# A batch in another order, with a query stack in the maxima's banks, merged ranks, and padding written in blocks during the attention

## The chip, the core and the metric

The kernel runs on one NeuronCore of a Trainium2 chip. The core has five engines, each with a program of its own, which meet only at semaphores: TensorE (PE: matmuls and transposes into PSUM), VectorE (DVE), ScalarE (ACT), GpSimd (POOL) and SyncE (SP), which here only issues DMAs. The metric is the device time of one execution in microseconds, as a median over runs. Lower is better.

## The reference

One layer with gated cross attention and a routed feed-forward part, in fp32, on 16 batches of 256 tokens with 256 features:

```python
x = x + tanh(g_xattn[0]) * attention(layernorm(x), ctx, ctx, ...)   # 16 heads of 16, softmax(q k / 4) v, then wo
x = x + tanh(g_ffn[0]) * ffn(layernorm(x), ...)
# ffn:
bids = sigmoid(x @ conf_w.T + conf_b) * wealth                # 8 experts
top_bids, selected = top_k(bids, 2)
routing_weights = softmax(top_bids)                           # over the two chosen
out = sum over the chosen experts of weight * (silu(x @ gate.T) * (x @ up.T)) @ down.T
```

## The kernel before

**Two stages.** The attention stage goes over the 16 batches; the expert stage goes over the tokens that were routed to each of the 8 experts. Between them lies a list of rows in DRAM, `dispatched`, with a region of 4096 + 256 rows of 272 floats for each expert: 256 normed features, 8 weights, the token's number. GpSimd scatters each batch's rows there with four indirect DMAs (L1211), to places that the routing has counted out. The expert stage reads a region in tiles of 256 rows, so what follows the last real row up to the end of its tile must be padding, rows of zero weight that point at a spare output row. The kernel before writes this padding in two ways: 32 rows at the head of each region early in the program (L435), and 256 rows behind the last real row of each, when the counts are known (`pad_experts`, L375, four experts by SyncE and four by GpSimd).

**A batch.** The program of an iteration `b` works on several batches at a time: scores, exps and weighing for `b`, the maxima (which are subtracted in the softmax) for `b + 1`, projections of Q and K for `b + 2`, output projection, residual and second layernorm for `b - 1`, ranks and rows of the dispatch for `b - 2`. The order is written out by hand, once for each engine, in a function `body`; the batches 0, 1, 14 and 15 are written out separately and the twelve between run in a loop of two. `ahead`, `nxt`, `back` and `late` say which of those parts an iteration has.

**PSUM.** `scores` holds one unit of work at a time: a pair of heads (`S0` to `S7`), or a stack of Q or K (`K0`, `K1`, `Q0`, `Q1`: the projection split into a high part and a rest, and put in the layout of heads). TensorE writes a unit, ScalarE reads it (exps or `read_stack`) and counts `unit_read`; TensorE's next unit waits for that. `maxps` holds the score maxima's own scores; VectorE reduces them (L984) and counts `max_taken`. `pv` holds the weighed values of one group of heads, which ScalarE copies out (`read_pv`, L818). `misc` has three banks that go round among all other products.

**The inputs of a batch.** SyncE loads the context (`load_ctx`, L394): batches 0 and 1 ahead of the loop, 2 in iteration 0, 3 and 4 in iteration 1, and then `b + 3` in iteration `b`. TensorE projects K of batch `b + 2` in iteration `b` (`project_k`, L493, for `b < 2`, from the load itself; later from a copy that GpSimd has split, `split_ctx`). At the end of iteration `b` SyncE moves the maxima's row into the queries of `b + 1` (`store_shift`, L422), for which `score(b + 1, 0)` waits. SyncE issues in the order of its program.

**From attention to experts.** After the last batch its rows are normed, routed and scattered, the counts are made (L1155), GpSimd adds the first outputs to `out` (`add_first`, L1884, one waiting for the other), SyncE loads the first full tile of rows (L1425), GpSimd copies it (L1882), and TensorE turns it (L1468) and begins gate and up (L1485).

## Time and profile before

| | before |
|---|---|
| time, median of 3 runs | 1084.73 us (1083.60 to 1086.69) |
| time of the profiled execution | 1083.07 us |
| its span from the first to the last instruction | 1081.4 us |
| TensorE busy, share of the span | 1001.3 us, 93% |
| VectorE, ScalarE, GpSimd busy | 610.8, 502.0, 366.3 us |
| mean traffic of the DMA engines | 71 GB/s |
| attention stage | up to about 444 us |
| first full tile of an expert begins | 483.24 us |

All times in rows are microseconds from the span's start. An engine's row tells when an instruction began, how long it took, the engine, the line, what it wrote from what, and in brackets how long the engine had been idle before it and what ended that. Ends of matmuls are modelled, so a small gap in TensorE is read from the starts. SyncE's rows are the issuing of DMAs, not their transfer.

### The profile page before, as it was taken

What the parts mean: (1) busy time and instruction counts of PE and PEld (TensorE: products, weight loads), DVE (VectorE), ACT (ScalarE), POOL (GpSimd) and SP (SyncE); (2) the same over time, 40 slices, a digit from 0 to 9 for tenths busy, and PEclk for the clock granted to TensorE, in tenths of its full rate; (3) what the DMA queues carried; (4) which work ended last, traced back from release to release, by engine and by line L of the source; (5) the groups of instructions that cost most, each with busy time, mean ns of one, the idle gap of its engine ahead of it and who ended that gap; (6) DMA issues with size and microseconds to landing.
All of it is one profiled execution on the core that took longest, in us unless ns stands there. A gap on an engine that the chain in (4) does not pass through costs nothing.

```text
span 1081.4 us, 25127 instructions
## 1 busy us (share of the span) xinstructions
PE 1001.3 (93%) x8750; PEld 855.2 (79%) x8750; DVE 610.8 (56%) x1519; ACT 502.0 (46%) x796; POOL 366.3 (34%) x439
## 2 busy tenths in 40 slices
PE   5789999999999997759999999999999999999993
PEld 4556777777777765448999999999799999999993
DVE  3556777777777776455544444444554444444452
ACT  4366777777777774334323232332433323233321
POOL 1124555555555552443322212121332212122121
PEclk8799999999999999869999999999999999999997
DMA  8000111111111119258712111121262212121211
GB/s 254 27 22 22 43 45 47 41 41 41 43 51 58 41 39 371 77 182 323 256 25 40 25 35 35 25 37 23 42 229 49 37 23 40 20 40 23 37 35 17
DMA packets 48338, 77.30 MB, mean 71 GB/s; under 512 B 8616, under 2 KB 42152, under 8 KB 44456
## 3 DMA queue, kind: packets, MB, share of 16 engines
q0 software_dynamic: 18080, 50.15, 16.7%
q1 hardware_dynamic: 30216, 26.62, 8.3%
q8 instruction: 23, 0.38, 0.1%
q14 instruction: 19, 0.16, 0.0%
HBM read 52.09 MB, written 24.40 MB: 71 GB/s over the span
## 4 chain that ended last, share of the span: by engine, by line
PE 81%; ACT 5%; issue 4%; DVE 3%; POOL 3%; DMA 1%; SPq 1%; POOLq 1%; ACTq 0%; DVEq 0%
PE gate L1485 17%; PE up L1485 17%; PE down L1499 11%; PE down L1501 6%; PE pv L590 4%; PE scores L579 4%; PE misc L486 4%; PE scores L540 3%; PE maxps L554 2%; PE misc L513 2%; PE misc L522 2%; POOL K_rest L1204 2%; ACT probs L771 1%; PE misc L624 1%; PE turned L1468 1%
## 5 line engine op out<-in xcount | busy, mean ns | idle before, releaser
L1937 POOL DMA_INDIRECT out<-y,token x64 | 100.9, 1577 | 424.8 <-DVE y L1806 323.8
L1696 ACT ACTIVATE silu<-gate 128x512 f32<-128x512 f32 x128 | 76.8, 600 | 281.6 <-PE up L1485 281.6
L984 DVE TENSOR_REDUCE max_neg<-maxps 128x4 f32<-128x1024 f32 x128 | 156.5, 1222 | 60.2 <-PE maxps L554 60.2
L1485 PE MATMUL gate<-x_hi,w_split 128*128 128x256 f32 x1024 | 185.0, 282 | 2.0 <-DVE x_lo L1772 1.6
L1797 DVE TENSOR_TENSOR h<-silu,up 128x512 f32<-128x512 f32 x128 | 88.1, 688 | 174.8 <-ACT silu L1696 174.8
L1499 PE MATMUL down<-w_split,h_hi 128*128 128x512 f32 x512 | 185.9, 398 | 0.0
L1485 PE MATMUL up<-x_hi,w_split 128*128 128x256 f32 x1024 | 184.4, 282 | 0.0
L771 ACT ACTIVATE probs<-scores 128x1024 f32<-128x1024 f32 x124 | 127.2, 1026 | 80.5 <-PE scores L579 79.5
L1485 PEld LDWEIGHTS gate<-x_hi,w_split 128*128 128x128 f32 x1024 | 149.4, 189 | 5.5 <-issue 2.7
L1485 PEld LDWEIGHTS up<-x_hi,w_split 128*128 128x128 f32 x1024 | 148.8, 189 | 0.0
L1501 PE MATMUL down<-w_split,h_lo 128*128 128x256 f32 x512 | 144.1, 281 | 0.0
L1799 DVE TENSOR_TENSOR h_lo<-h,h_hi 128x512 fp32r<-128x512 f32 x128 | 89.0, 696 | 89.5 <-ACT h_hi L1699 89.5
L1699 ACT ACTIVATE h_hi<-h 128x512 fp32r<-128x512 f32 x128 | 81.0, 633 | 96.8 <-DVE h L1797 96.8
L1499 PEld LDWEIGHTS down<-w_split,h_hi 128*128 128x128 f32 x512 | 96.2, 188 | 17.6
L1485 PE MATMUL up<-x_lo,w_split 128*128 128x256 f32 x512 | 103.2, 283 | 0.0
L1485 PE MATMUL gate<-x_lo,w_split 128*128 128x256 f32 x512 | 103.0, 283 | 0.0
L1501 PEld LDWEIGHTS down<-w_split,h_lo 128*128 128x128 f32 x512 | 96.4, 188 | 0.0
L1485 PEld LDWEIGHTS up<-x_lo,w_split 128*128 128x128 f32 x512 | 79.2, 189 | 0.0
L1485 PEld LDWEIGHTS gate<-x_lo,w_split 128*128 128x128 f32 x512 | 78.5, 189 | 0.0
L1211 POOL DMA_INDIRECT dispatched<-row,posi x64 | 63.9, 999 | 28.7 <-issue 17.3
L590 PE MATMUL pv<-probs,values 128*32 128x256 f32 x1024 | 69.4, 389 | 1.6 <-ACT oS L818 1.6
L579 PE MATMUL scores<-queries,keys 64*128 64x256 f32 x496 | 61.8, 328 | 8.3 <-ACT probs L771 4.3
(204 smaller groups left out, 1586.3 us busy)
## 6 DMA issues: line engine op xcount, KB each, us to landing
stage<-gate_up_T POOLq DMA_DIRECT2D x20, 1024.0 KB, 8.1
stage<-down_T POOLq DMA_DIRECT2D x10, 1024.0 KB, 11.1
xg<-dispatched SPq DMA_DIRECT2D x34, 272.0 KB
ctxT<-ctxT SPq DMA_DIRECT2D x17, 256.0 KB, 2.8
x_all<-x SPq DMA_DIRECT2D x16, 256.0 KB, 5.2
out<-x_all SPq DMA_DIRECT2D x16, 256.0 KB, 2.2
dispatched<-pads SPq DMA_DIRECT2D x4, 272.0 KB, 3.6
dispatched<-pads POOLq DMA_DIRECT2D x4, 272.0 KB, 4.3
```

Of the source, the lines that this page charges most:

```text
L579: last = mm(to[:, u * QT + t, :], k[par][r, pair, t * P:(t + 1) * P], q[par][r, pair, :], start=True, stop=True)
L590: last = mm(pv[j * SLOT:(j + 1) * SLOT, 0:SEQ], v[par][:, t, g * HPG + j, :], probs[g % 2][:, j, t, :], start=t == 0, stop=t == QT - 1)
L771: nc.scalar.activation(probs[g % 2][:, at:at + HPP].rearrange("p u t s -> p (u t) s"), home(b, pair), ACT.Exp).then_inc(s["unit_read"], 1)
L984: V.tensor_reduce(to, maxps[:], AX.X, ALU.max, negate=True).then_inc(s["max_taken"], 1)
L1485: last = mm(bank[:, i, :], into_inner(w, pair, mat)[:, c, cols], r[:, c, :], start=m == 0, stop=m == len(terms) - 1)
L1499: mm(down[t][:].rearrange("p (n d) -> p n d", n=2), h_hi[:, i, rows], split[:, :, cols], start=i == 0, stop=False, skip_group_check=True)
L1501: last = mm(down[t][:, 0:D], h_lo[:, i, rows], hi[:, cols], start=False, stop=i == IC - 1, skip_group_check=True)
L1696: nc.scalar.activation(silu[pair % 2][:], gate[pair % 2][:], ACT.Silu).then_inc(s_silu, 1)
L1699: nc.scalar.activation(h_hi[:, 2 * pair:2 * pair + 2, :], h[pair % 2][:], ACT.Copy).then_inc(s_hhi, 1)
L1797: V.tensor_tensor(h[pair % 2][:], silu[pair % 2][:], up[pair % 2][:], ALU.mult).then_inc(s_made, 1)
L1799: V.tensor_tensor(h_lo[:, 2 * pair:2 * pair + 2, :], h[pair % 2][:], h_hi[:, 2 * pair:2 * pair + 2, :].bitcast(fp32), ALU.subtract).then_i ...
L1937: pool.indirect_dma_start(out, bass.IndirectOffsetOnAxis(token[:, t:t + 1], axis=0), y[:, t, :], None, compute_op=ALU.add).then_inc(s_adde ...
```

## The change

Five things are changed together.

1. The padding. The 32 rows at the head of each region and the `pad_experts` at the end both go. Instead SyncE writes whole blocks of 256 rows in each of the 8 regions, from iteration 0 on: two blocks in iterations 0 and 1, one in each of 2 to 14, at the end of its `body` behind `store_shift`. A block is 8 DMAs of 272 KB. A scatter of batch `b` waits until `b + 1` blocks are written.
2. The order of an iteration from the fifth score on: `weigh(1)` goes ahead of `K0`, the Q projection ahead of score 5, `turn_x2` ahead of score 6, score 7 behind `weigh(2)`, `K1` behind the logits. ScalarE's order follows: `read_pv(1)` ahead of `K0`, `norm_x2` ahead of exps 5, `x2T` ahead of exps 7, the sigmoid ahead of `K1`. VectorE's `positions` go ahead of the sixth maximum.
3. The stack `Q0` goes to the banks of `maxps`, which are free once the maxima are turned. `Q1` then waits for the reading of `K1` alone.
4. The ranks of both token tiles are made by two matmuls of 16 columns in place of five of 8. For this VectorE adds the first tile's marks to the running count before the ranks (`macc[:, 1]`) and not behind them.
5. After the last batch, the first product of expert 2 is made ahead of turning the last rows, and the second between that and the logits; the counts' integer copy, which only the padding read, goes.

```diff
-            for e in range(EXPERTS):
-                sp.dma_start(disp[e * REGION:e * REGION + FIRST], pads[0:FIRST]).then_inc(s["first_rows_padded"], 16)
+
+            def pad_block(n):
+
+                rows = disp.rearrange("(e n) d -> e n d", e=EXPERTS)[:, bass.ds(n * SEQ, SEQ)].rearrange("e (t p) d -> p e t d", p=P)
+                for e in range(EXPERTS):
+                    sp.dma_start(rows[:, e], pads[:].unsqueeze(1).to_broadcast([P, QT, ROW])).then_inc(s["blocks_padded"], 16)
+
+            def pad_blocks(b):
+
+                if isinstance(b, int) and b < 2:
+                    pad_block(2 * b)
+                    pad_block(2 * b + 1)
+                elif isinstance(b, int) and b == BATCHES - 2:
+                    pad_block(BATCHES)
+                elif not is_last(b):
+                    pad_block(b + 2)
...
                 if nxt:
                     store_shift(b + 1, 1 - par, use)
+                pad_blocks(b)
...
-            return (lambda: store_residual(BATCHES - 1, EPILOGUE), lambda: pad_experts(sp, range(EXPERTS // 2)))
+            return (lambda: store_residual(BATCHES - 1, EPILOGUE),)
...
-            def stack(b, what, c, n):
+            def stack(b, what, c, n, to=None):
...
-                write_unit(n)
+                if to is None:
+                    to = scores
+                    write_unit(n)
...
-                for t in range(QT):
-                    mm(use.bank("RK")[:, t, 0:EXPERTS], before[:], m12[:, t, :], start=True, stop=False)
-                    if t == 1:
-                        mm(use.bank("RK")[:, t, 0:EXPERTS], ones[:], m12[:, 0, :], start=False, stop=False)
-                    last = mm(use.bank("RK")[:, t, 0:EXPERTS], ones[:], macc[:], start=False, stop=True)
-                last.then_inc(s["misc_written"], 1)
+                mm(use.bank("RK")[:, :, 0:EXPERTS], before[:], m12[:], start=True, stop=False)
+                mm(use.bank("RK")[:, :, 0:EXPERTS], ones[:], macc[:], start=False, stop=True).then_inc(s["misc_written"], 1)
...
+                weigh(b, par, 1)
                 stack_ahead("K0")
-                weigh(b, par, 1)
-                max_of_next(5)
-                score(b, par, 5)
                 if ahead:
                     project_q(use)
-                score(b, par, 6)
+                score(b, par, 5)
+                max_of_next(5)
                 if back:
                     turn_x2(b - 1, 1 - par, use)
+                score(b, par, 6)
                 max_of_next(6)
+                weigh(b, par, 2)
                 score(b, par, 7)
-                weigh(b, par, 2)
                 max_of_next(7)
-                stack_ahead("K1")
                 if back:
                     logits(use)
+                stack_ahead("K1")
                 if nxt:
                     turn_maxima(b + 1, use)
                 stack_ahead("Q0")
...
                 read_pv(b, 0)
                 if ahead:
                     read_whole(xT[:], "TX", use)
+                read_pv(b, 1)
                 stack_ahead("K0")
-                exps(b, 5)
                 if back:
                     norm_x2(b - 1, 1 - par)
-                read_pv(b, 1)
-                exps(b, 6)
+                exps(b, 5)
                 if ahead:
                     read_q(b + 2, use)
-                exps(b, 7)
+                exps(b, 6)
                 if back:
                     read_whole(x2T[:], "TX2", use)
+                exps(b, 7)
                 read_pv(b, 2)
-                stack_ahead("K1")
                 if back:
                     sigmoid(use)
+                stack_ahead("K1")
                 stack_ahead("Q0")
                 stack_ahead("Q1")
...
-                V.tensor_tensor(m12[:], m1[:], m2[:], ALU.add).then_inc(s["masks_ready"], 1)
+                V.tensor_tensor(m12[:], m1[:], m2[:], ALU.add).then_inc(s["masks_made"], 1)
+                dve.wait_ge(s["masks_made"], b + 1)
+                if not is_first(b):
+                    dve.wait_ge(s["rows_ready"], b)
+                V.tensor_tensor(macc[:, 1, :], macc[:, 0, :].bitcast(fp32), m12[:, 0, :].bitcast(fp32), ALU.add).then_inc(s["masks_ready"], 1)
...
                 max_of_next(4)
-                max_of_next(5)
                 if late:
                     positions(b - 2, par, use)
+                max_of_next(5)
                 max_of_next(6)
...
                 alone.wait_ge(s["rows_ready"], b + 1)
+                alone.wait_ge(s["blocks_padded"], b * (16 * EXPERTS) + 16 * EXPERTS)
...
             early_product(1, 1)
+            early_product(2, 0)
             turn_last_x2()
+            early_product(2, 1)
             last_logits()
-            early_product(2, 0)
-            early_product(2, 1)
             last_ranks()
```

## Rows read from the trace of the kernel before

**Rows 1.** Windows: stretch, length, busy us (instructions), granted clock, DMA share, GB/s.

```profile
16.00:28.00 12.00, 9.27 (x57) 6.84 (x56) 3.29 (x4) 7.26 (x12) 0.00 (x0) 0.72 0.92 295
...
48.15:54.95 6.80, 4.72 (x16) 3.46 (x16) 0.89 (x1) 0.42 (x2) 1.37 (x4) 0.50 0.13 40
...
98.30:398.00 299.70, 291.81 (x2823) 214.28 (x2821) 233.96 (x689) 223.12 (x348) 159.50 (x224) 1.00 0.13 43
404.70:421.40 16.70, 12.85 (x133) 8.11 (x131) 11.98 (x37) 8.59 (x15) 7.21 (x12) 1.00 0.98 404
467.50:475.50 8.00, 4.67 (x171) 4.01 (x162) 2.69 (x5) 4.28 (x5) 6.64 (x8) 0.71 0.94 323
474.80:488.40 13.60, 6.24 (x28) 5.88 (x29) 6.69 (x9) 2.60 (x3) 4.21 (x6) 0.50 0.73 236
```

**Rows 2.** Timeline of PE in the first batches: K projections of batches 2, 3.

```profile
50.23 3.78 PE L486 MATMUL misc<-ctxT,wk_s 128*128 128x256 f32 x8 [2.46 <-DMA ctxT<-ctxT]
...
77.16 1.99 PE L486 MATMUL misc<-ctxT,wk_s 128*128 128x256 f32 x8
```

**Rows 3.** Timeline of PE, first full tile of rows.

```profile
480.55 1.09 PE L1468 MATMUL turned<-idn,rows 128*128 128x128 f32 x4 [8.38 <-POOL rows L1882]
```

**Rows 4.** Timeline of SP in the first batches: issue of DMAs.

```profile
43.33 4.16 SPq L436 DMA_DIRECT2D dispatched<-pads  x8
...
70.63 1.33 SPq L427 DMA_DIRECT2D queries<-max_rows  x2
72.06 3.08 SPq L398 DMA_DIRECT2D ctxT<-ctxT  x2
```

**Rows 5.** Timeline of POOL between attention and experts.

```profile
470.13 2.94 POOL L381 DMA_DIRECT2D dispatched<-pads  x4
473.38 1.68 POOL L1885 DMA_INDIRECT out<-y_first,first_token  x1 [0.30 <-issue]
478.11 1.64 POOL L1885 DMA_INDIRECT out<-y_first,first_token  x1 [3.05 <-DMA out<-y_first,first_token]
479.52 0.88 POOL L1882 COPY rows<-xg 128x544 f32<-128x544 f32 x1
```

**Rows 6.** View of line 381, the large pads: issue in ns, landing in us.

```profile
L381 SPq DMA_DIRECT2D dispatched<-pads x4: 372/379/407, 466.7 to 470.6; - x4
...
DMA to landing us min/median/max: 2.3/4.2/4.8
```

**Rows 7.** View of line 388, the sixteen loads of x.

```profile
L388 SPq DMA_DIRECT2D x_all<-x x16: 434/469/925, 0.9 to 21.8; - x16
...
DMA to landing us min/median/max: 2.8/5.2/6.4
```

**Rows 8.** Timeline of PE in a full batch: five rank matmuls, K0.

```profile
235.61 0.25 PE L632 MATMUL misc<-m,before 128*128 128x8 f32 x1
...
236.06 0.25 PE L635 MATMUL misc<-macc,ones 128*128 128x8 f32 x1
236.66 0.39 PE L540 MATMUL scores<-K_high,picks_K high 64*128 64x256 f32 x2 [0.36 <-POOL K_rest L1204]
```

**Rows 9.** Timeline of ACT in the same batch.

```profile
236.10 0.38 ACT L818 ACTIVATE oS<-pv 128x256 f32<-128x256 f32 x1
...
237.44 1.11 ACT L778 ACTIVATE keys<-scores,ones_row 128x1024 fp32r<-128x1024 f32 x1 [0.47 <-PE scores L540]
...
240.07 1.08 ACT L794 ACTIVATE row<-x_all,shift,rstd 128x256 f32 x2
```

**Rows 10.** Timeline of PE in batch 14, where no K0 follows the ranks.

```profile
410.45 1.07 PE L590 MATMUL pv<-probs,values 128*32 128x256 f32 x16 [0.69 <-ACT oS L818]
```

**Rows 11.** DMA issues: count and median us from issue to landing.

```profile
out<-y_first,first_token POOLq DMA_INDIRECT x8, 3.2
```

**Rows 12.** Timeline of SP: loads of expert rows.

```profile
476.36 14.92 SPq L1425 DMA_DIRECT2D xg<-dispatched  x3
```

**Rows 13.** Timeline of DVE: splitting of weights before the first tile.

```profile
473.66 4.63 DVE L1811 TENSOR_TENSOR w_split<-stage,w_split 128x1024 fp32r<-128x1024 f32 x4 [1.05 <-ACT w_split L1710]
```

More of the change, by code:

```diff
@@ L287, in attention_stage @@
         STACKS = ["K0", "Q0", "K1", "Q1"]
+        BESIDE = "Q0"
         def units_before(b):
@@ L309, in home @@
             return scores[:]
+        beside = maxps[:].rearrange("p u t s -> p (u t) s")
         def first_stack_unit(b, what):
@@ L373, in attention_over @@
             eng.wait_ge(s["x2_stored"], 16 * BATCHES)
-        def pad_experts(eng, experts):
-            eng.wait_ge(s["pads_loaded"], 16)
-            eng.wait_ge(s["counted"], 1)
-            for e in experts:
-                n = eng.value_load(counts[0:1, e:e + 1], min_val=0, max_val=TOKENS)
-                eng.dma_start(disp[bass.ds(n + e * REGION, TILE)].rearrange("(t p) d -> p t d", p=P),
-                              pads[:].unsqueeze(1).to_broadcast([P, TT, ROW])).then_inc(s_padded[2 * e // EXPERTS], 16)
         def sync_attention(sp):
@@ L539, in stack @@
                             r = slice(half * STACK, (half + 1) * STACK)
-                            last = mm(scores[:, half * QT + i, :], picks[f"{what} {part}"][r, i, :], source[what][r, c, :],
+                            last = mm(to[:, half * QT + i, :], picks[f"{what} {part}"][r, i, :], source[what][r, c, :],
                                       start=part == "high", stop=part == "rest")
@@ L641, in known_counts @@
                 use.free(pe, "KNOWN")
-                mm(use.bank("KNOWN")[:, 0, 0:EXPERTS], ones[:], macc[:], start=True, stop=True).then_inc(s["misc_written"], 1)
+                mm(use.bank("KNOWN")[:, 0, 0:EXPERTS], ones[:], macc[:, 0, :], start=True, stop=True).then_inc(s["misc_written"], 1)
             pe.wait_ge(s["first_loaded"], 16 * NFIRST)
@@ L680, in stack_ahead @@
                 def stack_ahead(what):
-                    if ahead:
-                        stack(b + 2, what[0], int(what[1]), unit(b, what))
+                    if ahead and what == BESIDE:
+                        stack(b + 2, what[0], int(what[1]), None, beside)
+                    elif ahead:
+                        stack(b + 2, what[0], int(what[1]), unit(b, what) - (1 if UNITS[UNITS.index(what) - 1] == BESIDE else 0))
                 if isinstance(b, int) and b < 2:
@@ L752, in count_rows @@
                 EPILOGUE2.free(pe, "COUNT")
-                mm(EPILOGUE2.bank("COUNT")[:, 0, 0:EXPERTS], ones[:], macc[:], start=True, stop=True).then_inc(s["misc_written"], 1)
+                mm(EPILOGUE2.bank("COUNT")[:, 0, 0:EXPERTS], ones[:], macc[:, 0, :], start=True, stop=True).then_inc(s["misc_written"], 1)
             pe.wait_ge(s["w_split"], 2)
@@ L869, in stack_ahead @@
                     if ahead:
-                        read_stack(par, what[0], int(what[1]), unit(b, what))
+                        read_stack(par, what[0], int(what[1]), unit(b, what), beside if what == BESIDE else None)
                 exps(b, 0)
@@ L1032, in positions @@
                 dve.wait_ge(s["second_ready"], b + 1)
-                link = chain(dve, "rows_chain", 14, b, behind=1)
+                link = chain(dve, "rows_chain", 13, b, behind=1)
                 link(V.tensor_tensor(t8[:], m1[:], u8[:], ALU.mult))
@@ L1156, in count @@
                 EPILOGUE2.written(dve, "COUNT")
-                link = chain(dve, "count_chain", 2, 0)
-                link(V.tensor_copy(counts[:], EPILOGUE2.bank("COUNT")[:, 0, 0:EXPERTS]))
+                link = chain(dve, "count_chain", 1, 0)
                 link(V.tensor_scalar(tiles[:], EPILOGUE2.bank("COUNT")[:, 0, 0:EXPERTS], float(TILE - 1 - FIRST), None, ALU.add))
@@ L1258, in scatter_last @@
                 scatter(BATCHES - 1, (BATCHES - 1) % 2)
-                pad_experts(pool, range(EXPERTS // 2, EXPERTS))
             over_batches(pool, body)
```

33 lines of the change are left out of this document (14 added, 19 removed).

## Prediction

> **What bounds the kernel now.** I read the windows first. In the twelve full batches in the middle (98.3 to 398 us) TensorE is busy 291.81 of 299.70 us, at the full clock (1.00), against 234, 223 and 160 us for VectorE, ScalarE and GpSimd [rows 1]. A batch takes 24.98 us, TensorE waits in 0.66 us of it, and no other engine comes near. So in a full batch the order of TensorE's work is worth at most its waits, plus matmuls that vanish. Then I read TensorE's timeline for longer waits. There are two that the change touches: 2.46 us before the K projection of batch 2, for a context load [rows 2], and 8.38 us between the attention and the first full expert tile, for GpSimd's copy of the rows [rows 3]. SyncE's timeline says why the first exists: the load of batch 2's context stands behind eight pad writes that take 4.16 us to issue [rows 4]. GpSimd's says why the second does: pads, two accumulating writes one after the other, then the copy [rows 5]. Durations are from the profiled execution, 1083.07 us for a span of 1081.4; the median of the runs is 1.66 above it. About 0.3% (3.25 us) can be told from no change.
>
> **First batches, what is removed.** The eight small pad writes (43.33 to 47.49) go, so the load of context 2 is issued 4.2 us earlier and has landed before TensorE asks: -2.46 [rows 2, 4]. The half clock (1.2 GHz, 0.50) of 48.15 to 54.95 lies around that wait, and TensorE is busy 4.72 of its 6.8 us [rows 1]. The same projection took 3.78 us there and 1.99 at 2.4 GHz [rows 2]. If the clock stays up, at most another 2.2 us return; if not, nothing. I take 0.8. Sum: -3.3 (-2.5 to -4.7).
>
> **First batches, what is added.** This decides the sign. `pad_blocks(0)` writes two blocks, 16 DMAs of 272 KB, right after the shift rows of batch 1 (issued 70.63 to 71.96). The very next thing in SyncE's program is `load_ctx(3)`, now issued at 72.06 [rows 4], and TensorE projects K of batch 3 at 77.16 [rows 2]. A context load is there 2.6 us or so after its issue (issued right behind 47.49, it releases TensorE at 50.23) [rows 2, 4], so today there are some 2.5 us to spare. With 16 pads ahead:
> issue alone: 0.379 us each [rows 6], 16 make 6.1, so the load is issued at 78.1 and lands at 80.6: 3.4 us late even if the pads' bytes took no time.
> bytes: 16 x 278.5 KB = 4.46 MB. SyncE's transfers land in the order of issue and pile up: of the 16 loads of x the last was issued at 21.8 and landed 6.4 us later, where the quickest took 2.8 [rows 7]. The stretch in which these 1 KB rows stream moved 295 GB/s with the DMA engines 0.92 busy; the one in which today's large pads and scatters run, 323 at 0.94; the expert weights' large rows, 404 at 0.98 [rows 1]. The pads are rows of 1088 bytes, so 323 is nearest. A lone pad lands after 2.3 us [rows 6], the other fifteen at 0.86 each, the context behind them 0.81: 72.0 + 2.3 + 12.9 + 0.8 = 88.0, or 10.8 us after 77.16. With 404 GB/s it is 8.1, with 295 12.2.
> The Trainium skill says the same in "DMA: Bandwidth & Descriptors", "Queues, rings and completion order": all DMAs issued by SyncE share one row of rings, and each DMA engine consumes its ring in order. The piling up of the loads of x agrees [rows 7]. Its "Specifications" give about 358 GB/s per core for HBM; by that the fifteen pads would take 11.7 instead of 12.9 us, and the stall be 9.5.
> TensorE's program is in order, so the scores, the weighing and all later work of batch 1 stand behind `project_k(3)`. Both shifts move together, so the -3.3 doesn't change the stall. After such a wait TensorE comes back at 1.2 GHz: the window from 474.8 to 488.4 is at 0.50 throughout, and covers the second half of the 8.38 us wait and 7.9 us after it [rows 1, 3]. 3 to 7 us at a pace 1.9 times slower lose 1.5 to 3.4; I take 2.4. Sum: +13.2 (9.6 to 15.6). Batch 2 gets two blocks as well, but the context load behind them is for GpSimd's split near the end of that batch, over 20 us after its issue, as in all later batches, where 8 pads (6.9 us) lie ahead of it. The residual's store behind them is read by nobody until the end. Scatters now wait for their blocks, which were issued two batches before: nothing.
>
> **Full batches.** Five rank matmuls, 0.11 us apart, become two [rows 8]: -0.33. K0 waits 0.36 us for K_rest [rows 8]; behind `weigh` it won't. But `weigh(1)` now stands directly behind the ranks, and needs the bank that ScalarE empties at 236.10 + 0.38 = 236.48 [rows 9]. With the hand-over that is 236.6, and the pair of K0 and `weigh` starts at 236.66 today [rows 8]: both gains sink into a new wait of some 0.8 us. The trace has this order already, in batch 14, which has no K0: `weigh` behind the ranks waits 0.69 us for ScalarE's oS [rows 10]. What follows: K0 goes from about 237.6, its eviction starts 0.78 later as now (236.66 to 237.44) and takes 1.11, then `norm_x2`, which now stands before exps(5), takes 1.08 [rows 9], to 240.5. score(5), behind K0 (0.67) and the Q projection (1.92), is at 240.2; its exps runs from about 240.8 to 241.8, and score(6), for which TensorE is free at 241.5, waits 0.3. Against these stand the waits that go: 0.2 or so for Q1, since Q0 has banks of its own, and smaller ones. I take 0.0 per batch, between -0.2 and +0.3, for twelve -2.4 to +3.6. At the far end, if every wait of TensorE went and the ranks too, it would be 0.66 + 0.33 a batch, -12. The extra VectorE sum ahead of the ranks has its cover in the same wait; without it it would cost its own length. `positions` ahead of max 5 runs while TensorE projects Q. In batches 14 and 15 the same trades occur once each, and block 16 competes with the last weight loads: +0.3 (-0.5 to +1).
>
> **Between attention and experts.** GpSimd loses four pads, 2.94 us from 470.13 [rows 5]; its first accumulating write starts at 470.4, lands after 3.2 us, the median of these writes [rows 11], instead of 4.0 without pads in the way, the second follows at 474.3, and 1.4 later the copy: 475.7 instead of 479.52. SyncE's row load (476.36) no longer waits for pads, only for the last scatter, and is issued by 473.5 [rows 12]. Then the tile could start 3.8 earlier. The first x_lo needs VectorE, which splits weights until 478.29 [rows 13]; with the turn at 476.7 and ScalarE's copy behind it x_lo is due at 478.6, so that just fits. -3.8 (-2.5 to -4.2). A shorter wait also means fewer matmuls at 1.2 GHz, or the same: -0.6 (-1.5 to +1, with the moved early products, which only fill a wait of TensorE). The two fewer rank rounds and one count fewer on the last batch's chain are offset by the extra sum: -0.1. Sum -4.5.
>
> **The sum**: -3.3 + 13.2 + 0.0 + 0.3 - 4.5 = +5.7 on 1083.07, so 1088.8 for a profiled execution and 1090.4 as a median.
>
> **Rivals.**
> (1) The pads get out of the way: the load of context 3 comes only as late as the issue makes it. For it: 404 GB/s has been moved. Against: not with rows of 1 KB. Stall 3.4, clock 1.5: 1084.73 - 3.3 + 4.9 + 0.3 - 4.5 = 1082.1, inside what can't be told or just below.
> (2) The new order pays, on the other side: if `weigh(1)` didn't wait for oS, each batch would lose its 0.8 us and TensorE would go through, 12 x 0.8 = -9.6: 1080.8. It decides from 0.75 us a batch on (9.0/12, with 5.7 to make good and 3.25 to be told). For it: TensorE is the bound in every batch. Against: batch 14 shows the wait, and ScalarE's order ahead of that eviction is unchanged.
> (3) The pads disturb every batch: 2.2 MB stream in the first 9 us of each, after the shift rows (the wait for which isn't seen in any full batch) and beside scatters. If the shift rows came late by 0.5 us a batch: +6, 1096. For it: they are on the same DMA engines. Against: the pads are issued behind them.
>
> **How the numbers follow.** Forecast 0.60, with its own range of 1085 to 1096; rival (1) 0.15, (2) 0.12, (3) 0.13. The time is the forecast's, 1090.4. The range takes in most of (1) and (3) and half of (2): 1081 to 1098. Faster by over 0.3%: (2) and a third of (1), 0.16. The same: the rest of (1) and the low end of the forecast, 0.20. Slower: 0.64.
>
> **What would show it.** In the changed profile: no wait before the K projection of batch 2; before that of batch 3 a wait of 8 to 12 us for ctxT, TensorE at 0.50 behind it; batches of 24.7 to 25.2 us with a wait of 0.6 to 0.9 for oS before `weigh(1)` and none for K_rest; the wait before the first row turn down from 8.38 to 4 to 5 us. I am wrong if context 3 lands in time, or if a full batch changes by over 0.3 us.

## The result

The change made the kernel slower: 1100.93 us as a median of four runs (1097.48 to 1103.49) against 1085.71 (1083.60 to 1087.39) on the same chip, a ratio of 1.0144 with a 95% interval of 1.0118 to 1.0171. 1090.4 was predicted, with 1098 as the upper end. The profiled execution of the changed kernel took 1097.48 us with a span of 1095.7, 14.3 above the span of before. Four stretches, each from one mark on TensorE's timeline to the next, hold all of it: V of batch 2 is the first V of a full batch, "heads" is the start of the last group of transposes of `oS`, "gate" the first product of the first full tile.

| stretch | before | after | difference | predicted |
|---|---|---|---|---|
| start to V of batch 2 | 98.27 | 109.17 | +10.9 | +9.9 |
| twelve full batches | 299.73 | 302.47 | +2.7 | 0.0 |
| V of batch 14 to the heads of batch 15 | 45.19 | 50.45 | +5.3 | +0.3 |
| heads of batch 15 to the first gate | 40.05 | 35.69 | -4.4 | -4.5 |
| the rest | 598.2 | 597.9 | -0.2 | 0 |

The windows of the changed kernel, columns as in [rows 1]: the wait before K of batch 3 with what follows it, the full batches, batches 14 and 15, and the way to the first gate.

```profile
76.00:89.60 13.60, 4.32 (x14) 3.14 (x16) 0.00 (x0) 0.00 (x0) 0.00 (x0) 0.50 0.65 209
109.17:411.64 302.47, 290.17 (x2786) 211.97 (x2784) 234.62 (x688) 223.18 (x348) 160.15 (x224) 1.00 0.41 139
411.64:462.09 50.45, 36.26 (x310) 24.00 (x308) 24.92 (x90) 24.84 (x38) 20.56 (x30) 0.83 0.88 322
462.09:497.78 35.69, 20.40 (x339) 14.63 (x340) 20.88 (x91) 11.79 (x21) 14.98 (x18) 0.78 0.21 59
```

In the full batches TensorE is busy 1.7 us less than in [rows 1] (fewer rank matmuls) and the stretch is 2.7 us longer: its waits grew. In batches 14 and 15 the granted clock is 0.83.

The timeline of TensorE of the changed kernel, at the places of [rows 2], [rows 8], [rows 10] and [rows 3], and at the first score of batch 15:

```profile
47.27 1.99 PE L492 MATMUL misc<-ctxT,wk_s 128*128 128x256 f32 x8
...
85.28 3.78 PE L492 MATMUL misc<-ctxT,wk_s 128*128 128x256 f32 x8 [11.74 <-DMA ctxT<-ctxT]
...
248.50 1.07 PE L598 MATMUL pv<-probs,values 128*32 128x256 f32 x16 [0.65 <-ACT oS L824]
...
253.71 0.50 PE L587 MATMUL scores<-queries,keys 64*128 64x256 f32 x4 [0.29 <-ACT probs L777]
...
439.00 0.80 PE L587 MATMUL scores<-queries,keys 64*128 64x256 f32 x4 [5.34 <-DMA queries<-max_rows]
...
495.09 1.09 PE L1473 MATMUL turned<-idn,rows 128*128 128x128 f32 x4 [5.34 <-POOL rows L1887]
```

The wait for context 2 [rows 2] is gone, that for context 3 is new, `weigh(1)` waits for `oS` in every batch, and K0 no longer waits for `K_rest`. SyncE's timeline of the same execution tells why context 3 is late. Its issue is the row behind the sixteen pads:

```profile
67.25 1.32 SPq L418 DMA_DIRECT2D queries<-max_rows  x2
68.61 11.64 SPq L431 DMA_DIRECT2D dispatched<-pads  x16
80.35 5.33 SPq L389 DMA_DIRECT2D ctxT<-ctxT  x2
...
411.51 5.97 SPq L431 DMA_DIRECT2D dispatched<-pads  x8
422.90 0.40 SPq L445 DMA_DIRECT2D out<-x_all  x1
433.14 1.36 SPq L418 DMA_DIRECT2D queries<-max_rows  x2
```

```profile
488.18 1.61 POOL L1890 DMA_INDIRECT out<-y_first,first_token  x1 [0.30 <-issue]
492.00 1.63 POOL L1890 DMA_INDIRECT out<-y_first,first_token  x1 [2.21 <-DMA out<-y_first,first_token]
494.11 0.83 POOL L1887 COPY rows<-xg 128x544 f32<-128x544 f32 x1 [0.48 <-DMA xg<-dispatched]
```

### The profile page after: what moved, and what is told of

Same layout as the page of the kernel before. It is cut to its first block, busy times and chain, and to the rows that moved or that the text cites. A ratio compares the mean times of both kernels' runs of the same rounds, so it can differ in the third digit from the quotient of the medians.

```text
span 1095.7 us, 25472 instructions
## 1 busy us (share of the span) xinstructions
PE 999.1 (91%) x8702; PEld 852.4 (78%) x8702; DVE 611.9 (56%) x1518; ACT 502.2 (46%) x796; POOL 363.3 (33%) x435
## 4 chain that ended last, share of the span: by engine, by line
PE 80%; ACT 6%; issue 5%; DVE 3%; DMA 2%; SPq 2%; POOL 1%; ACTq 0%; DVEq 0%; POOLq 0%
PE gate L1490 17%; PE up L1490 17%; PE down L1504 11%; PE down L1506 6%; PE pv L598 6%; PE scores L587 4%; PE misc L492 4%; PE scores L548 3%; PE maxps L562 2%; ACT probs L777 2%; PE misc L519 2%; PE misc L528 2%; PE turned L1473 1%; PE misc L480 1%; ACT xn L791 1%
## 5 line engine op out<-in xcount | busy, mean ns | idle before, releaser
L587 PEld LDWEIGHTS scores<-queries,keys 64*128 64x128 f32 x496 | 38.0, 190 | 47.7 <-ACT probs L777 20.8
```

The lines of the kernel that those rows point to most:

```text
L587: last = mm(to[:, u * QT + t, :], k[par][r, pair, t * P:(t + 1) * P], q[par][r, pair, :], start=True, stop=True)
```

## The experiments

All marks are those of the table above: V of batch 2, the mean of ten periods (V of batch 4 to V of batch 14), batches 14 and 15 with TensorE's mean granted clock in them, and the tail. Ratios are to the kernel before on the same chip; a dash is a single execution.

| kernel | median us | ratio, 95% | V of batch 2 | period | 14 and 15 (clock) | tail |
|---|---|---|---|---|---|---|
| before | 1085.71 | | 98.27 | 24.88 | 45.19 (0.92) | 40.05 |
| after | 1100.93 | 1.0144 (1.0118-1.0171) | 109.17 | 25.16 | 50.45 (0.83) | 35.69 |
| pads only | 1093.75 | 1.0076 (1.0050-1.0102) | 108.78 | 24.85 | 49.52 (0.83) | 38.32 |
| order only | 1089.72 | 1.0047 (1.0033-1.0062) | 96.05 | 25.16 | 49.31 (0.80) | 41.05 |
| after, context 3 ahead | 1085.14 | 1.0006 (0.9991-1.0020) | 96.07 | 25.16 | 51.98 (0.81) | 36.56 |
| after, half the bytes | 1097.08 | - | 105.08 | 25.15 | 52.93 (0.78) | 36.62 |
| after, pads moved | 1095.23 | 1.0093 (1.0076-1.0110) | 93.40 | 25.17 | 49.80 (0.81) | 36.45 |
| before, pads moved | 1091.34 | 1.0057 (1.0035-1.0078) | 93.95 | 24.88 | 49.38 (0.79) | 36.72 |
| order, statistics later | 1098.23 | 1.0124 (1.0099-1.0149) | 98.35 | 26.09 | 45.45 (0.92) | 40.58 |
| early products only | 1085.81 | 0.9998 (0.9985-1.0012) | 98.68 | 24.88 | 45.17 (0.92) | 40.08 |
| context 2 first | 1080.51 | 0.9964 (0.9947-0.9980) | 97.29 | 24.87 | 47.35 (0.86) | 40.40 |
| before, pads spread | 1076.75 | 0.9924 (0.9902-0.9946) | 93.32 | 24.87 | 47.86 (0.82) | 36.79 |
| ranks only | 1085.65 | 1.0006 (0.9990-1.0021) | 98.87 | 24.86 | 47.39 (0.89) | 40.40 |
| order, no ranks | 1090.12 | 1.0050 (1.0033-1.0067) | 97.21 | 25.16 | 48.61 (0.83) | 41.37 |

**Pads only.** The kernel before with the blocks of padding (`pad_block`, `pad_blocks`, the wait ahead of the scatter, no `pad_experts`) and nothing else of the change.

> The kernel before with the blocks of padding alone; order, stacks and ranks stay. Theory A (the pads stand in front of other transfers of SyncE's queue and beside the weight loads of batches 14 and 15): a wait of 10 to 13 us for context 3 in batch 1, full batches of 24.9 us as before, some 5 us lost around batches 14 and 15, some 4 us won between attention and experts: 1097 us. Rival B (the new order of a batch is what costs): about the kernel before or faster, 1080 to 1086.

TensorE's timeline:

```profile
85.06 3.78 PE L489 MATMUL misc<-ctxT,wk_s 128*128 128x256 f32 x8 [11.41 <-DMA ctxT<-ctxT]
```

The wait before K of batch 3 is 11.41 us, so the blocks alone make it. The full batches keep their period (24.85), though each now moves 2.2 MB of pads: beside the attention these bytes cost nothing that a full batch shows. Batches 14 and 15 lose 4.3 us. The tail gains 1.7 where theory A had 4, and the time is 1093.75 where it had 1097.

**Order only.** All of the change but the padding.

> The kernel before with the new order, the stack in the maxima's banks and the merged ranks; padding as before. Theory A: full batches of 25.1 to 25.2 us in place of 24.9, so 3 us over twelve, no wait for context 3, the wait of 8.4 us before the first full tile stays: 1087 to 1090. Rival B: most of the 15 us is here, 1097 or more. Rival C (the pads' traffic is what makes full batches longer, and the order gains): batches of 24.9 us or less.

The whole +0.28 us a batch is here, and no wait for a context. The medians come near to adding up: 9.3 us of the first and 5.3 of this one against 15.2 of both. By stretches they don't: batches 14 and 15 lose 4.3 and 4.1 us apart and 5.3 together, and the tail changes by -1.7 and +1.0 apart and by -4.4 together. So the agreement of the medians is partly luck.

**Context 3 ahead of the pads,** in the changed kernel:

```diff
-                    sp.wait_ge(s["misc_written"], use.before)
-                    load_ctx(b + 2, par)
+                    if b == 0:
+                        sp.wait_ge(s["misc_written"], use.before)
+                        load_ctx(b + 2, par)
...
                 if nxt:
                     store_shift(b + 1, 1 - par, use)
+                if is_first(b):
+                    sp.wait_ge(s["misc_written"], ITER1.before)
+                    load_ctx(3, 1)
                 pad_blocks(b)
```

> The changed kernel, with context 3 loaded in iteration 0 ahead of the 16 pads and not behind them. Theory A: the wait for context 3 (11.7 us) and the half clock behind it are gone, 12 to 14 us: 1087 to 1089. Rival D (the pads' bytes disturb TensorE's transfers wherever they stand): context 3 still comes some 5 to 10 us late, 1095.

One DMA moved past sixteen others takes 13.1 us off the first batches (V of batch 2 at 96.07, not 109.17). The profiled execution falls by 10.4 us, to 1087.12, since batches 14 and 15 take 1.5 us more and the tail 0.9. The median falls by 15.8, to that of before. Of that, 5.4 us is not in the two profiles: the profiled run of after is the quickest of its four, and the one here lies 2.0 above the median of its ten. So the move is worth 10 to 13 us, and the rest of the change still costs 3.9 us in this profile (a span of 1085.3 against 1081.4). Timelines of SyncE and TensorE in this kernel, where the same sixteen pads now follow:

```profile
69.47 0.39 SPq L389 DMA_DIRECT2D ctxT<-ctxT  x1
69.91 11.97 SPq L431 DMA_DIRECT2D dispatched<-pads  x16
```

```profile
74.26 0.92 PE L496 MATMUL misc<-ctxT,wk_s 128*128 128x256 f32 x3
```

K of batch 3 starts at 74.26 with no wait. The pads themselves are unchanged, so it is the place in SyncE's order that costs, not the traffic beside the engines. Context and pads land in the order in which they were issued, the context at 72.32 and the pads from 73.19 to 86.40. With this the trace agrees with the Trainium skill, "DMA: Bandwidth & Descriptors", "Queues, rings and completion order", where each DMA engine takes what one issuing engine put in its ring in order.

**Half the bytes, as many DMAs.** Iteration 0 writes one block in sixteen DMAs of 136 KB, iteration 1 the other three, and the scatters wait for one block's worth of DMAs more:

```diff
+                if isinstance(n, int) and n == 0:
+                    for e in range(EXPERTS):
+                        for t in range(QT):
+                            sp.dma_start(rows[:, e, t], pads[:]).then_inc(s["blocks_padded"], 16)
+                    return
...
```

> The changed kernel, with 16 pad DMAs of half the size in iteration 0 (block 0 alone, in halves; block 1 follows in iteration 1). If the bytes in the queue make context 3 late, as predicted, the wait falls from 11.7 us to 5 to 6. If the number of DMAs does (issue), it stays at 10 to 12.

SyncE's and TensorE's timelines:

```profile
68.48 9.41 SPq L433 DMA_DIRECT2D dispatched<-pads  x16
77.99 3.28 SPq L389 DMA_DIRECT2D ctxT<-ctxT  x2
```

```profile
80.86 1.65 PE L500 MATMUL misc<-ctxT,wk_s 128*128 128x256 f32 x3 [7.47 <-DMA ctxT<-ctxT]
```

The wait is 7.47 us, between what half the bytes alone and the unchanged count alone would give. The small pads are issued and land 0.5 us apart (0.43 to 0.46 for an issue, but for the seventh of 2.02, whose cause the trace doesn't show), nearly all 1.9 to 2.2 us after their issue. The large ones pile up: the first lands after 2.3 us, the thirteenth after 4.1. So with 272 KB the draining sets the pace, with 136 KB the issuing. The prediction's two bounds, issue and bytes, are both real, and the larger one counts.

**Pads moved, in the changed kernel and in the kernel before.** Context 3 ahead of all pads; then blocks 0 and 1; 2, 3 and 4 in iteration 1 and `b + 3` in iteration `b`, from iteration 1 on ahead of the residual's store and the shift rows; none in batches 14 and 15.

```diff
...
+                if b != 0 if isinstance(b, int) else True:
+                    pad_blocks(b)
                 if back:
                     store_residual(b - 1, use)
                 if nxt:
                     store_shift(b + 1, 1 - par, use)
-                pad_blocks(b)
...
```

> The changed kernel with its padding blocks placed elsewhere in SP's order: context 3 is loaded ahead of all pads, every batch's pads stand ahead of its residual store and its shift rows and one batch earlier (blocks 0 and 1 in batch 0; 2, 3 and 4 in batch 1; block b+3 in batch b), so that none is issued in batches 14 and 15. Theory (a): the pads' traffic in batches 14 and 15 delays the x2 store and with it the shift rows of batch 15; without it the stretch from V of batch 14 to the heads of batch 15 falls from the 51.98 us of the kernel with context 3 ahead to the 49.3 of the new order alone, the wait of the first score of batch 15 falls from 5.57 to about 2.2 us, and the time is about 1082.5 us. Theory (b): the loss in batches 14 and 15 is the new order's and the clock's; the stretch stays at 51 to 52 us and the time at 1085. The mean period of the full batches stays at 25.15 to 25.16 us by both.

> The order of the kernel before, with only the padding blocks of the change and these placed as in the mended form (context 3 ahead of all pads, pads one batch earlier and ahead of the residual store and the shift rows, none in batches 14 and 15). Theory (a): the blocks cost nothing in the full batches (24.85 to 24.88 us a batch), save some 2.8 us in the first batches (K of batch 2 at about 47.4 instead of 50.23), nothing more is lost in batches 14 and 15 (45.2 us from V of batch 14 to the heads of batch 15, as before), and the tail from there to the first gate takes 38.3 instead of 40.05 us: together -4.5 us, 1080 us. Theory (b): the pads disturb batches 13 to 15 wherever they stand in SP's order, or the time won early is given back where the weight loads end: 1084 to 1088 us.

Both forecasts of the time missed, since I had made the same mistake again one place further on. Timelines of SyncE and TensorE in the second of the two:

```profile
80.48 18.75 SPq L428 DMA_DIRECT2D dispatched<-pads  x24
99.27 0.64 SPq L444 DMA_DIRECT2D out<-x_all  x1
99.95 1.51 SPq L415 DMA_DIRECT2D queries<-max_rows  x2
```

```profile
106.31 0.79 PE L590 MATMUL scores<-queries,keys 64*128 64x256 f32 x4 [10.68 <-DMA queries<-max_rows]
```

Twenty-four pads now stand ahead of the shift rows of batch 2, and the first score of batch 2 waits 10.68 us (11.10 in the other kernel). It also failed in batches 14 and 15: with no pad issued there the stretch still takes 49.38 us in this kernel, at a clock of 0.79, where theory (a) had 45.2. In the changed kernel theory (a) came close there: the wait of the first score of batch 15 fell to 2.12 us and the stretch from 51.98 to 49.80, for 49.3. Both windows are at a clock of 0.81, so the pads' traffic in these batches costs about 2.2 us.

**Statistics later.** Order only, with `stats_x(b + 2)` behind `max_of_next(0)` on VectorE.

> The new order and merged ranks without the padding blocks (1089.72 us), with one edit on VectorE: the LayerNorm statistics of x two batches ahead (five instructions, 1.6 us) move from ahead of the reading of V and the first maxima to behind the first maxima. Theory (a): the chain on VectorE over the batch boundary (turned maxima, first choice, statistics, V, first maxima) sets when the second maxima's matmuls may begin, so the period of a full batch falls from 25.155 to between 24.9 and 25.05 us and the time to 1086.5 to 1088.5 us. Theory (b): the period is set inside the batch by ScalarE's read of the first attention output ahead of the weighing (0.65 us wait) and by the exponentials; then what is won at the boundary is lost at that wait, the period stays within 0.03 of 25.155 and the time within 1 us of 1089.7.

Neither held: the period grew to 26.09. The timelines of VectorE show why, first of order only, then of this kernel:

```profile
270.58 0.41 DVE L994 CAST max_rows<-misc 16x256 fp32r<-16x256 f32 x1 [0.75 <-PE misc L567]
...
274.50 0.25 DVE L940 BATCH_NORM_AGGREGATE mv<-stats 128x2 f32<-128x6 f32 x2 [0.26 <-DVE stats L935]
274.66 0.74 DVE L979 TENSOR_TENSOR values<-misc,bv_s 128x256 f32<-128x256 f32 x2
```

```profile
226.69 0.41 DVE L994 CAST max_rows<-misc 16x256 fp32r<-16x256 f32 x1 [0.75 <-PE misc L567]
...
228.75 0.17 DVE L1012 TENSOR_TENSOR m<-u,r 128x16 f32<-128x16 f32 x1
230.56 0.76 DVE L979 TENSOR_TENSOR values<-misc,bv_s 128x256 f32<-128x256 f32 x2 [1.64 <-PE misc L525]
231.23 1.23 DVE L987 TENSOR_REDUCE max_neg<-maxps 128x4 f32<-128x1024 f32 x1
232.38 0.42 DVE L935 BATCH_NORM_STATS2 stats<-x_all 128x6 f32 x1
```

V isn't made yet when the first choice is done. The statistics had filled a wait of VectorE for TensorE, and behind the maxima they delay the second ones: TensorE waits 0.7 us for VectorE's maxima in eleven batches, where order only has one such wait. VectorE takes V 3.87 us after the turned maxima (the cast at 226.69) here, and 4.08 in order only, so its chain holds TensorE there by 0.2 us at most; it is not what a move of 1.6 us can mend.

**Ranks only, and the order without the ranks.** The two halves of the trade inside a batch.

> The kernel before with the merged ranks alone (two rank matmuls a batch for five, and one sum more on VectorE). Theory (a): what TensorE saves, 0.33 us a batch, goes into the wait for K_rest behind it (0.36 to about 0.69 us), the period stays at 24.87 us within 0.03 and the time within 1.5 us of 1085. Theory (b): the saved matmuls shorten the batch by 0.33 us, twelve times 4 us: 1081.

> The new order of a batch with the query stack in the maxima's banks, without the merged ranks and without the padding blocks. Theory (a): the period of the new order is set by ScalarE's read of the first attention output and by the exponentials behind it, so that three more rank matmuls only fill the wait of 0.65 us before the weighing (0.3 left): the period stays at 25.13 to 25.17 us and the time within 1.5 us of the 1089.7 of the order with merged ranks. Theory (b): TensorE's own work sets it: 25.45 to 25.5 us and about 1093.5.

Theory (a) held both times. TensorE's timeline of ranks only, then of the order without the merged ranks:

```profile
237.19 0.39 PE L540 MATMUL scores<-K_high,picks_K high 64*128 64x256 f32 x2 [0.68 <-POOL K_rest L1203]
```

```profile
236.47 1.07 PE L595 MATMUL pv<-probs,values 128*32 128x256 f32 x16 [0.31 <-ACT oS L825]
```

Three rank matmuls less turn 0.36 us of waiting for `K_rest` [rows 8] into 0.68. Three more turn 0.65 us of waiting for `oS` into 0.31. The period doesn't move in either, so those matmuls lay in a wait both before and after.

**Early products only.** The kernel before with the last edit of the change (item 5) and nothing else.

> The kernel before with only the last edit of the change: the turn of the last x2 and the last logits stand one place later among the early products of the experts on TensorE. Theory (a): the tail's gain in the changed kernel comes from this move and the padding together; alone it lets TensorE run up the clock ahead of the logits but the wait for the counts and the shared pad stores remains, so the time is 1083 to 1085 us with 39 to 40 us from the heads of batch 15 to the first gate. Theory (b): the move alone makes the gain: 36 to 37 us for that stretch and 1080.5 to 1081.5 us. Theory (c): it delays the last logits by a product (about 2 us) and nothing gives it back: 1086 us.

Nothing is won: 40.08 us of tail. That is theory (a); the time, 1085.81, lies 0.8 above its range and within 0.2% of before.

**Context 2 first.** The kernel before, with one move on SyncE:

```diff
-            for e in range(EXPERTS):
-                sp.dma_start(disp[e * REGION:e * REGION + FIRST], pads[0:FIRST]).then_inc(s["first_rows_padded"], 16)
...
                     load_ctx(b + 2, par)
+                    if b == 0:
+                        for e in range(EXPERTS):
+                            sp.dma_start(disp[e * REGION:e * REGION + FIRST], pads[0:FIRST]).then_inc(s["first_rows_padded"], 16)
```

> The kernel before with one move on SP: the load of context 2 stands ahead of the eight first-row pads instead of behind them. Nothing is added and nothing is left out, so that only the wait of 2.46 us before the K projection of batch 2 goes. Both theories: K of batch 2 at about 47.4 instead of 50.23 us and everything up to V of batch 14 some 2.5 to 4.5 us earlier. Theory (a): batches 14 and 15 are held by the transfers beside them, which don't change, so they take 45.2 us from V of batch 14 to the heads of batch 15 as before, and the time falls by 2.5 to 4.5 us, to 1080.6 to 1082.6. Theory (b): in batches 14 and 15 TensorE's clock is what moves, and it comes out otherwise as soon as the same work comes some us earlier or later, with no transfer added: that stretch takes 47 to 50 us, and the time stays within 2 us of 1085.

Faster by 0.36%, with no wait for context 2. V of batch 14 comes 1.1 us earlier in the profiled execution, not 2.5 to 4.5. The median, 1080.51, is near theory (a). Yet in the profiled execution, of 1083.96 us, batches 14 and 15 took 47.35 us at 0.86, as theory (b) had it, with no transfer added anywhere. Six of its twelve runs took 1078.86 to 1079.23 us, with a granted clock of 0.969 to 0.972 over the whole run, and six 1081.79 to 1084.34, with 0.962 to 0.967, the profiled one among the latter.

**Pads spread.** The order of before, with the blocks behind loads that are due and ahead of nothing that is: 0 and 1 behind context 2, block 2 behind context 3, 3 and 4 behind context 4, then `b + 3` behind the context load of iteration `b`.

```diff
...
                     load_ctx(b + 3, 1 - par)
+                    pad_block(b + 3)
...
```

> The order of the kernel before with the padding blocks of the change where SP has nothing behind them that is due: blocks 0 and 1 right behind context 2, block 2 behind context 3, blocks 3 and 4 behind context 4, block b+3 behind the context load of batch b, none in batches 14 and 15. By the theory that only what stands behind the pads in SP's order is late, no context and no shift rows are waited for in the first four batches (V of the first full batch at 93.5 to 94 us, 4.5 us earlier than before), the period stays 24.88 us, and the tail from the heads of batch 15 to the first gate takes 36.7 to 38.3 us instead of 40.05. With 45.2 us in batches 14 and 15 that gives 1077 to 1079 us; with the 49.4 us that the two kernels with pads and the old order took there, 1081 to 1083. Rival: 4.46 MB of pads between 43 and 56 us disturb batch 1 itself: over 1086.

1076.75 us, 0.76% faster than before, the fastest kernel of this study. Its windows: full batches, batches 14 and 15, the tail, and the stretch at half clock in batches 14 and 15.

```profile
93.32:392.93 299.61, 291.75 (x2823) 214.30 (x2821) 234.02 (x689) 223.13 (x348) 159.23 (x224) 1.00 0.41 132
392.93:440.79 47.86, 38.47 (x316) 25.27 (x314) 24.87 (x89) 24.62 (x38) 21.10 (x31) 0.82 0.64 246
440.79:477.58 36.79, 22.50 (x345) 15.51 (x346) 20.29 (x91) 11.80 (x21) 15.71 (x19) 0.80 0.21 61
411.40:428.40 17.00, 15.11 (x93) 9.22 (x86) 6.60 (x26) 6.86 (x10) 5.61 (x7) 0.50 0.79 312
```

The rival didn't come: 4.46 MB of pads between 43 and 60 us delay nothing. The first batches give 4.95 us, the tail 3.3, and batches 14 and 15 take 2.7 back.

**Four kernels profiled again,** to learn whether the program or the execution sets the clock in batches 14 and 15.

> The kernel before, unchanged, profiled once more. In its first profile batches 14 and 15 took 45.19 us from V of batch 14 to the heads of batch 15 at a mean granted clock of 0.92. Theory (a): the stretch is fixed by the program: 45.1 to 45.3 us at 0.92 again. Theory (b): TensorE's clock comes out otherwise from execution to execution: any length from 45 to 49 us, with the same waits and a clock of 0.79 to 0.92.

> The changed kernel, unchanged, profiled once more; its first profile had 50.45 us in batches 14 and 15 at a granted clock of 0.83, and a wait of 5.34 us of the first score of batch 15 for its shift rows. Theory (a): 50.2 to 50.7 us again. Theory (b): 48 to 54 us with the clock; the wait for the shift rows stays between 4.3 and 5.6 us, since the transfers make it. By both the wait of 11.7 us before the K projection of batch 3 and the period of 25.16 us stay within 0.3 and 0.02.

> The kernel before with context 2 ahead of the first-row pads, profiled once more; its first profile took 1083.96 us with 47.35 us in batches 14 and 15 at 0.86, while six of its twelve runs took 1078.9 to 1079.2. Theory (a): 47.3 us again. Theory (b): the clock differs: about 45.2 us at 0.92 where the run is one of 1079 us, 47 to 48 where it is one of 1082 to 1084.

> The new order and merged ranks without the padding blocks, profiled once more; its first profile had 49.31 us in batches 14 and 15 at a granted clock of 0.80. Theory (a), the new order itself costs 4 us there: 49.3 us again. Theory (b), it costs 0.3 us at an equal clock: 45.4 us where the clock is 0.92, 48 to 50 where it is 0.80 to 0.83. By both the period is 25.155 us within 0.02.

| kernel | first profile | second profile |
|---|---|---|
| before | 45.19 (0.92) | 45.67 (0.93) |
| after | 50.45 (0.83) | 51.95 (0.81) |
| context 2 first | 47.35 (0.86) | 47.31 (0.86) |
| order only | 49.31 (0.80) | 49.76 (0.81) |

The two profiles of one program lie within 1.5 us of each other, where the programs lie between 45 and 52. So much of the stretch comes with the program. Neither theory holds alone, though: before and after missed the narrow ranges of theory (a), and the other two kernels came back at the clock of their first profiles, where both theories say much the same. That executions of one program differ too is told by the granted clock of whole runs: the kernel before, on the chip of context 2 first, took from 1081.59 us at 0.972 to 1088.98 at 0.964. The second profile of the changed kernel has its waits again: 11.76 us for context 3, 5.59 for the shift rows. By stretches, the second profile of after against that of before gives +7.4, +2.7, +6.3 and -3.2 us, so batches 14 and 15 are again far from the +0.3 that was predicted.

## Why the prediction was right and wrong

**First batches: right.** +9.9 predicted, +10.9 measured. Context 3 behind sixteen pads was the step that decided the sign, and with that one load moved the first batches lose nothing. The stall was put at 10.8 us from bytes at 323 GB/s and came to 11.74; the K projection behind it ran at 1.2 GHz for 3.78 us as the one of [rows 2] does. Rival (1), that the issue at 0.379 us each is all that counts, fell with it. One part went another way than was thought: the load does not leave SyncE after 6.1 us to wait for the bytes ahead of it, it is issued 11.7 us after the first pad and lands 4.9 after that, since the bytes hold the issuing itself. A first sign of this stood in [rows 7], where one issue took 925 ns against a median of 469. The pads went at 304 GB/s on the mean, at 353 once one landed every 0.79 us. That the sum came within 1 us has some luck in it: from K of batch 2 on the two pairs of profiles give +13.9 and +12.8 us, but ahead of it -3.0 and -5.4, of which 1.2 and 2.2 are there at the first turned maxima, ahead of the pads that were taken out.

**Between attention and experts: right as a sum,** -4.5 and -4.4, but not part by part. The wait ahead of the row turn went from 8.38 to 5.34 us, 3.0 of the 3.8 predicted. Early products alone give nothing and pads alone 1.7 us, yet the kernels with the blocks gain 3.3 to 4.4 where the mean clock of the tail is 0.78 to 0.83, and 1.7 where it is 0.73, near the 0.72 of before. So the gain goes together with TensorE's clock, though not with it alone: early products only has 0.77 there and gains nothing. How the gain divides isn't shown.

**Full batches: the step was right and its size was not.** The predicted waits are there: `weigh(1)` waits 0.65 us for `oS` (0.8 predicted), score 6 waits 0.29 for the exps (0.3), and the wait for `K_rest` is gone. The term of 0.0 was mis-sized: it measured +0.28 us a batch, +2.7 over the twelve, inside the bound of +3.6. Start to start on TensorE's timeline, one batch of before (24.88 us) against one of order only (25.13): ranks with the wait behind them -0.04 and Q1 -0.19, both as predicted; the two units behind K0 -0.04; the turn of x2 with scores 6 and 7 and the maxima between +0.15, half of what was predicted. Not foreseen were +0.21 from the last maxima to Q0, and +0.16 at the second maxima: there TensorE hands back most of what Q1 won, since VectorE reads V behind its statistics, 4.08 us after it took the turned maxima, where V is there after 3.87 (statistics later). What the +0.21 waits for, in gaps too small for a row, isn't settled. Rival (2), TensorE going through, fell. So did rival (3): with the blocks alone the period is 24.85.

**Batches 14 and 15: the step that failed,** "the same trades occur once each, and block 16 competes with the last weight loads: +0.3 (-0.5 to +1)". It measured +5.3. Without those 5.0 us the median would have been 1095.9, inside the range. The step counted matmuls and one transfer, block 16, and took the clock of before for granted. Two things came in its place.

The first is a transfer. In the changed kernel the pads of block 15 run into GpSimd's six weight loads; the store of the residual, issued at 422.90, lands only at 437.16 (9.8 us after its issue in before, 14.3 here), the shift rows behind it come late too, and score 0 of batch 15 waits 5.34 us where it waited 2.63. Without pads in these batches it waits 2.12. Views of the store, before and after, and the score of before and of pads moved in the changed kernel:

```profile
L440 SPq DMA_DIRECT2D out<-x_all x16: 383/390/425, 84.8 to 449.7; - x16
DMA to landing us min/median/max: 2.1/2.2/9.8
```

```profile
L445 SPq DMA_DIRECT2D out<-x_all x16: 383/384/421, 95.0 to 468.6; - x16
DMA to landing us min/median/max: 2.1/2.2/14.3
```

```profile
423.11 0.50 PE L579 MATMUL scores<-queries,keys 64*128 64x256 f32 x4 [2.63 <-DMA queries<-max_rows]
```

```profile
433.79 0.50 PE L595 MATMUL scores<-queries,keys 64*128 64x256 f32 x4 [2.12 <-DMA queries<-max_rows]
```

That is 2 to 3 us: 3.2 by the wait, 2.2 by the two stretches at a clock of 0.81.

The second is the clock. Windows of V of batch 14 to the heads of batch 15, of before, of pads moved in the order of before (no pads there), of order only and of statistics later (no pads either):

```profile
398.00:443.19 45.19, 34.78 (x316) 23.23 (x314) 24.89 (x89) 24.51 (x38) 21.29 (x31) 0.92 0.69 264
```

```profile
405.63:455.01 49.38, 40.05 (x315) 25.97 (x313) 24.95 (x89) 24.62 (x38) 21.17 (x31) 0.79 0.62 239
```

```profile
398.46:447.77 49.31, 38.52 (x309) 24.69 (x308) 25.04 (x90) 24.94 (x38) 20.58 (x30) 0.80 0.63 239
```

```profile
411.47:456.92 45.45, 34.01 (x310) 22.64 (x308) 25.05 (x90) 24.72 (x38) 20.57 (x30) 0.92 0.68 259
```

The first two have the same instructions in the same order, and the second moves no more bytes there; TensorE is busy 5.3 us longer with them, since it spent 20.5 of the 49 us at 1.2 GHz, not 6.8. The last has the new order and the merged ranks and takes 45.45 us at a clock of 0.92. So at an equal clock the new order costs 0.3 us there, what the prediction had, and the rest of its 4 us is the clock. In the changed kernel the same instructions keep TensorE busy for 36.26 us, 2.2 more than in this last window. Most of its time at half clock is one stretch:

```profile
434.40:448.00 13.60, 8.43 (x47) 5.66 (x48) 4.39 (x23) 4.16 (x5) 1.67 (x3) 0.50 1.05 383
```

TensorE had stood idle since 433.66, in the wait for the shift rows, when the clock fell. So the two causes may not be independent here: +5.3 is 0.3 of the order, 2 to 3 of the wait, and the rest, 2 to 3, the clock, part of which the wait may have brought. Context 2 first moves one load on SyncE, some 370 us earlier, and its stretch is 2 us longer in both profiles. What in the timing tips the clock isn't shown. Six runs of that kernel were about 3 to 5 us quicker without any change, and had the higher clock; in which stretch they had it isn't on record.

In sum: 1.0 of the miss is in the first batches, 2.7 in the full ones, 5.0 in batches 14 and 15, and the median lies 3.5 us above the profiled execution, where 1.7 was taken. The profiled one was the quickest of the four runs, at a granted clock of 0.963, and the others had 0.957 to 0.962. Two small sums of the prediction are off and move nothing: the loss by the clock is 1.4 to 3.3 us by its own pace, not 1.5 to 3.4, and the parts of "faster" add up to 0.17.

## What to carry to other kernels

Before a bulk of DMAs is put on an engine, look for the next small load in that engine's program and when it is due: sixteen large writes hold it up by their draining or their issuing, whichever is longer, though one place later the same writes didn't delay it at all. Matmuls that lie in a wait are not worth removing until the wait goes, and work that fills another engine's wait should stay where it is. In a stage where TensorE waits a fifth of the time, sum the clock apart from the waits, because an edit far ahead of it can move the one and not the other, and take more than one execution, because those of one program differ there too.

## What was not expected of the hardware

SyncE's issue of a 272 KB write took 0.38 us when few were under way and 0.73 when the ones ahead were draining, so the issuing engine itself is held, and not only the transfer. A store of 256 KB whose median landing is 2.2 us took 14.3 beside the weight loads and pads. And one and the same stretch of attention took between 45.2 and 52.9 us over these kernels, at granted clocks from 0.93 to 0.78; at an equal 0.81 it was 49.80 without pads in it and 51.98 with them.
